# Projections of the next chunk moved inside the recurrence of the current one, recurrence in half steps, and three smaller edits

## What is computed

```python
# 1. state space block (the mixer)
h = rmsnorm(x); xi, z = split(h @ in_proj.T)             # 2 x 512 columns
xi = silu(causal_conv(xi, 4 taps))
dt, B, C = split(xi @ x_proj.T)                          # 16 + 16 + 16
delta = softplus(dt @ dt_proj.T + b); A = -exp(A_log)    # 512 channels, 16 states
s = s * exp(delta*A) + delta*B*xi                        # over tokens
y = (sum over states of s*C + xi*D) * silu(z)
x = layernorm(2*x + y @ out_proj.T)
# 2. cross attention: 8 heads, rotary on q and k, 2 x 64 keys, then relu(norm(.) @ W_ffn)
x = layernorm(x + xattn(x, ctx))
# 3. mixture of experts: one shared and 8 routed, top 2 by softmax
x = layernorm(x + sum_e c_e * (silu(x @ w1_e + b1) * (x @ w3_e + b3)) @ w2_e)
```

## Time and profile before

| | us |
|---|---|
| median of 2 runs (lowest, highest) | 1169.16 (1169.08, 1169.25) |
| profiled execution: its own time, its span | 1168.82, 1167.0 |
| busy in the span: PE, DVE, ACT, POOL | 916.1, 828.9, 545.8, 535.4 |

### The profile page before, as it was taken

The page is one execution under the profiler, slowest core; times in us unless marked ns, Lnnn a source line. Parts: engine busy times, 40 slices in busy tenths (PEclk is TensorE's granted clock), DMA queues, the critical chain, the costliest instruction groups (busy, mean ns, idle before and its releaser), DMA issues.

```text
span 1167.0 us, 13071 instructions
## 1 busy us (share of the span) xinstructions
PE 916.1 (79%) x4208; PEld 697.8 (60%) x4208; DVE 828.9 (71%) x1222; ACT 545.8 (47%) x1015; POOL 535.4 (46%) x318
## 2 busy tenths in 40 slices
PE   4857688486788998486788998477789985767996
PEld 2446673265677883265677883265678872645885
DVE  1699964698999954698999954698999961213233
ACT  3556736453455526453455526453555512413342
POOL 1267710743468720743468720743468723001552
PEclk9979999796689999796689999796689996755998
DMA  5111102101033302101033302102033212001330
GB/s 202 38 36 55 37 1 74 54 19 64 28 104 114 92 10 92 54 19 64 28 102 112 95 10 92 54 19 64 28 100 103 88 36 91 0 1 37 102 123 29
DMA packets 37714, 71.96 MB, mean 62 GB/s; under 512 B 3856, under 2 KB 12185, under 8 KB 37647
## 3 DMA queue, kind: packets, MB, share of 16 engines
q1 hardware_dynamic: 37646, 71.13, 18.9%
HBM read 64.62 MB, written 2.30 MB: 57 GB/s over the span
## 4 chain that ended last, share of the span: by engine, by line
PE 28%; issue 20%; POOL 19%; DVE 13%; ACT 5%; POOLq 0%; DMA 0%; DVEq 0%; ACTq 0%; SPq 0%
POOL dbu L537 11%; PE ps L928 8%; PE ps L1005 5%; DVE hs L1111 3%; POOL work L572 3%; PE ps L902 3%; PE ps L759 2%; DVE yacc L1164 2%; PE ps L848 2%; POOL w_lo L564 2%; DVE mx L1260 2%; POOL work L558 2%; POOL work L554 2%; PE ps L842 1%; ACT work L707 1%
## 5 line engine op out<-in xcount | busy, mean ns | idle before, releaser
L537 POOL TENSOR_TENSOR dbu<-v,bbc 128x1024 f32<-128x1024 f32 x128 | 301.8, 2364 | 218.0 <-DVE v L1097 124.4
L1111 DVE TENSOR_TENSOR_SCAN hs<-ps,carry,dbu 128x512 f32<-128x512 f32 x256 | 312.9, 1265 | 0.6 <-PE ps L759 0.6
L645 ACT ACTIVATE ps<-delta,neg_a 128x512 f32<-128x512 f32 x256 | 175.2, 691 | 174.0 <-DVE hs L1111 174.0
L759 PE MATMUL ps<-ident,hs 128*128 128x128 f32 x1024 | 161.2, 303 | 65.9 <-DVE yacc L1164 47.5
L759 PEld LDWEIGHTS ps<-ident,hs 128*128 128x128 f32 x1024 | 133.8, 158 | 90.5 <-DVE hs L1111 64.1
L564 POOL TENSOR_TENSOR w_lo<-w13s,w_hi 128x512 fp32r<-128x512 f32 x72 | 93.4, 1297 | 130.4 <-ACT w_hi L734 129.2
L1164 DVE SCALAR_TENSOR_TENSOR yacc<-ps,ctok,yacc 128x512 f32<-128x512 f32 x210 | 147.3, 737 | 1.9 <-PE ps L759 1.0
L1005 PE MATMUL ps<-w2s,work 128*128 128x256 f32 x576 | 136.3, 380 | 0.3
L747 ACT ACTIVATE work<-ps,half_b 128x512 f32<-128x512 f32 x72 | 49.6, 689 | 143.8 <-PE ps L928 139.8
L1005 PEld LDWEIGHTS ps<-w2s,work 128*128 128x128 f32 x576 | 105.8, 190 | 14.9 <-DVE work L1282 1.5
L928 PE MATMUL ps<-x_hi,w_hi 128*128 128x512 f32 x288 | 108.4, 458 | 7.6 <-DVE work L1282 7.3
(11 more groups left out here) (169 smaller groups left out, 1322.4 us busy)
## 6 DMA issues: line engine op xcount, KB each, us to landing
w13s<-in_w SPq DMA_DIRECT2D x72, 256.0 KB, 2.9
bbc<-brow_dram SPq DMA_DIRECT2D x32, 512.0 KB, 4.0
w2s<-in_w SPq DMA_DIRECT2D x36, 256.0 KB, 2.7
cbc<-comb_dram SPq DMA_DIRECT2D x32, 256.0 KB, 3.5
work<-work SPq DMA_DIRECT2D x16, 256.0 KB, 2.3
xn<-in_x SPq DMA_DIRECT2D x4, 512.0 KB, 4.7
xt<-in_x SPq DMA_DIRECT2D x4, 512.0 KB, 4.8
rope<-in_rope_q SPq DMA_DIRECT2D x4, 512.0 KB, 5.4
```

What stands on the lines that cost most here:

```text
L537: pool.tensor_tensor(dbu[:, i % DRING, :, :], v[:, 2 * h:2 * h + 2, :], bbc[:, n // 2 % 2, n % 2, :].rearrange("p (o t) -> p o t", o=1) .t ...
L645: act.activation(ps[:, unit % 2, :], delta[:, q, :], ACT.Exp, scale=neg_a[:, q * NS + m:q * NS + m + 1]).then_inc(da_done.sem, 1)
L759: last = pe.transpose(ps[:, bank, t * P:(t + 1) * P], src(t), ident[:, :])
L1111: dve.tensor_tensor_scan(hs[:, m % 2, q, 0:TC], ps[:, unit % 2, :], dbu[:, n % DRING, q % 2, :], carry[:, m, q:q + 1], ALU.mult, ALU.add). ...
```

## The change

The list is written anew. A recurrence now has 70 **half steps**, each with one unit and one sum. The `pre` steps of chunks 1 to 3 become twelve steps `ahead` 0 to 11, which stand inside the recurrence of the chunk before: in the first recurrence three half steps apart, later at the ticks 12 to 22 of the second stream, of 1.5 half steps each (attention ticks have 1, expert ticks 2). They use two or four PSUM banks and the buffer `work`, so their results (`u`, `sz`, `delta`, `v`, 1 MB each) are stored in DRAM (`kept`) and loaded back by `load` 0 to 2 towards the end of the recurrence and after `post` 3. Ticks of the second stream that don't fit in a recurrence are `left`: some stand at the boundary between two recurrences, two of them (`INSIDE`) in the next one.

The three smaller edits: the expert weights are split once, in the first recurrence, and the parts kept in DRAM, from where each chunk loads both (512 KB a half instead of 256 KB, ring of 4 instead of 3); the scores' factor is put in the keys, so that one reduction with `negate` gives `top` and L1263 goes; `gm` becomes `(b + b3)*gac` in PSUM and `hh = (th + 1)*gm`, so that neither has two operands in SBUF.

```diff
+UNITS = NS * Q
+STEPS = UNITS + 6
+WAITS = (1, 1, 1, 1, 1, 1, 1, 1, 1, 1, 1, 1, 1.5, 1.5, 1.5, 1.5, 1.5, 1.5, 1.5, 1.5, 1.5, 1.5, 1.5)
+LEFT_W, FIRST_W, FFN_W, INSIDE = 2, 4, 2, 2
...
+        for h in range(STEPS):
+            steps.extend(early[h] + mixer(i, "sum", h) + mid[h] + mixer(i, "scan", h) + late[h])
+            if h == STEPS - 8:
+                steps.extend(mixer(i + 1, "load", 0))
...
+    items = [only(3, mixer(0, "split", n)) for n in range(3)]
+    items += [only(3, mixer(1, "fetch", n) + mixer(0, "split", n + 3)) for n in range(4)]
+    items += [only(3, mixer(1, "ahead", n) + mixer(0, "split", n + 7)) for n in range(AHEAD)]
...
+        steps += mixer(i - 1, "post", 0) + mixer(i - 1, "post", 1) + mixer(i - 1, "post", 2) + mixer(i, "begin", 0)
+        steps += mixer(i - 1, "post", 3) + mixer(i, "load", 2)
...
+                if kind == "load" and n == 0:
+                    sp.wait_ge(*dbu_done.at(j, 0))
+                    sp.wait_ge(*dv_kept.at(j - 1, 128))
+                    sp.dma_start(v[:, :, :], kept["v"].rearrange("q p t -> p q t")).then_inc(v_in.sem, 16)
...
-                sp.dma_start(w13s[:, c % HRING, :, :, :].rearrange("p s k n -> p (s k n)"), w13[c]
-                             ).then_inc(w13_in[c % HRING].sem, 16)
+                sp.wait_ge(*b_ps.at(j, max(0, c - HRING + 1)))
+                for dst, src in ((w13_hi, hi_dram), (w13_lo, lo_dram)):
+                    sp.dma_start(dst[:, c % HRING, :, :, :].rearrange("p s k n -> p (s k n)"), src[c]
+                                 ).then_inc(w13_in[c % HRING].sem, 16)
...
+                    if c == 0 and j + 2 < CHUNKS:
+                        pe.wait_ge(*delta_done.at(j + 2, Q))
...
-                        dve.tensor_reduce(mx[:, :], s8, AX.X, ALU.max).then_inc(mx_done.sem, 1)
-                        dve.tensor_scalar(top[:, :], mx[:, :], -HD ** -0.5, None, ALU.mult
+                        dve.tensor_reduce(top[:, :], s8, AX.X, ALU.max, negate=True).then_inc(top_score_done.sem, 1)
...
-                    dve.scalar_tensor_tensor(out=gm[:, ib, :], in0=th[:, ib, :], scalar=1.0,
+                    dve.wait_ge(*b_ps.at(j, c + 1))
+                    dve.scalar_tensor_tensor(out=ps[:, 5, :], in0=ps[:, 5, :], scalar=col("b3", c),
                                              in1=(gac if c >= 2 else ga)[:, ib, :],
                                              op0=ALU.add, op1=ALU.mult).then_inc(gm_done.sem, 1)
```

More of the change, by code:

```diff
@@ new lines, in mixer, with second, tick, round_of @@
+    def mixer(chunk, *what):
+        return [("mixer", chunk, *what)] if 0 <= chunk < CHUNKS else []
+    def second(chunk, t, *parts):
+        return [("second", chunk, part, t) for part in parts]
+    def tick(chunk, t, weight, more=()):
+        return weight, second(chunk, t, "early"), second(chunk, t, "mid"), second(chunk, t, "late") + list(more)
+    def round_of(i, items):
+        early, mid, late = ([[] for _ in range(STEPS)] for _ in range(3))
+        at = 0.0
+        for weight, e, m, l in items:
+            start, end = int(at), max(int(at), int(at + weight) - 1)
+            early[start] += e
+            mid[start] += m
+            late[end] += l
+            at += weight
+        assert at <= STEPS, at
+        for h in range(STEPS):
+            steps.extend(early[h] + mixer(i, "sum", h) + mid[h] + mixer(i, "scan", h) + late[h])
+            if h == STEPS - 8:
+                steps.extend(mixer(i + 1, "load", 0))
+            if h == STEPS - 6:
+                steps.extend(mixer(i + 1, "load", 1))
@@ L104, in schedule @@
+    steps += mixer(CHUNKS - 1, "post", 0) + mixer(CHUNKS - 1, "post", 1) + mixer(CHUNKS - 1, "post", 2)
+    for n in range(max(3, len(left))):
+        steps += mixer(CHUNKS - 1, "post", 3 + n) if n < 3 else []
+        steps += second(CHUNKS - 2, left[n], "early", "mid", "late") if n < len(left) else []
+    for t in range(T_OUT + 1):
+        steps += second(CHUNKS - 1, t, "early", "mid", "late")
     return steps
@@ L1099, in mixer @@
[L1099 to L1102 removed]
+                    tokens_of_c(j, 7)
+                    soft_start(j, range(Q))
+                if kind == "pre" and n == 6:
+                    soft_end(j, (0, 1))
+                    soft_end(j, (2, 3))
+                if kind == "sum" and 6 <= n < UNITS + 6:
+                    sum_states(j, *divmod(n - 6, NT))
@@ L1103, in mixer @@
+                if kind == "scan" and n < UNITS:
+                    for unit in (n,):
                         m, q = divmod(unit, Q)
```

540 lines of the change are left out of this document (381 added, 159 removed).

## The result

| | us |
|---|---|
| before, median of 2 runs (lowest, highest) | 1169.16 (1169.08, 1169.25) |
| after, median of 2 runs (lowest, highest) | 1299.94 (1299.63, 1300.25) |
| ratio, 95% interval | 1.1112 (1.1088 to 1.1136) |
| forecast, range | 1136 (1082 to 1190) |

The account below looks back on a forecast made before the run. Neither DVE (215.6) nor PE (214.1) fills a 262.8 us round; the gap moves between stages. 61.8 + 135.8 + 259.7 + 253.7 + 210.2 + 213 = 1134.2 us of span, forecast 1136, range 1082 to 1190.

Parts of the forecast that it names:

- What the change takes out of DVE: DVE's work per round: L1263 saves 5 us and `gm` 8 us, so 215.6 becomes 203.
- What moves, work and lock: Projections moved into the recurrence: 19.6 us of DVE work a chunk, plus 5 us of waiting beside POOL.
- third rival: DVE and POOL lock paid in full: 16 instructions wait 2.1 us each, 34 us a chunk, 1217 us; chance 0.07.
- First recurrence: First scan to gate's end: 106.2 plus 19.6 + 5 moved and 5 for waits, 135.8 us; splits and DMAs hide.
- Start and rotary step: Start of each round: 18.8 + 25.6 us in round 1, 6.3 + 25.6 in rounds 2 and 3; rotary step uncovered.
- Tiles: Attention tiles: PE is late at 7.6 us a tile, 32 us in rounds 1 and 2, 30 in round 3.
- Ticks 12 to 22: Norms, gate and projections: 73 us in rounds 1 and 2, between 64 overlapped and 90 in a row; 34.5 in round 3.
- second rival: In ticks 12 to 22 the two chains run one after the other, 90 us instead of 73 twice, 1170 us; chance 0.20.
- Experts: Expert ticks: PE bounds at 5.35 us each, 85.6 us in round 1, 96.3 in round 2; DVE bounds round 3, 106.7.
- Boundary: Between two recurrences: 24.7 us from last sum to chunk 2's first scan, 11 idle on DVE; 20.5 in round 2.
- fourth rival: A store or load comes late at each boundary, 5 to 10 us a round; a stall dear as the lock had 0.05.
- The rest: From chunk 3's output projection to the end: 215.1 us before becomes 213.

Follow-up runs that it names:

- e4_two_edits: The kernel before with only the one reduction with negate and `gm` in PSUM; median of five runs 1149.5 us against 1170.1, ratio 0.9824.
- e5_wide_ahead: The kernel after with 2.5 half steps in place of 1.5 in each of ticks 12 to 22; 1298.6 us.
- e1_no_ahead: The kernel after without `ahead`, its `fetch` and the stores and loads of results, chunks 1 to 3 using what chunk 0 left; 1149.9 us.

## Why the prediction was wrong, step by step

**What the change takes out of DVE: right.** `gm` has come down to 0.73 to 0.76 us, and `e4_two_edits` alone gains 10.3 us in each of the first two rounds.

**What moves, work and lock: right.** 25.8 us of DVE in the first recurrence against my 24.6. The group of convolution instructions in after, beside POOL:

```profile
L1431 DVE SCALAR_TENSOR_TENSOR work<-work,vec 128x512 f32<-128x512 f32 x36 | 39.0, 1148 | 3.3 <-ACT work L861 3.1
```

1.15 us each instead of 0.75 makes 14.4 us in three chunks, 4.8 a chunk; I took 5. `v` takes 0.90 us on average and costs no more than before's 0.96. The rule on the lock (the Trainium skill, "SBUF — State Buffer", section "Who interferes with whom") names the mechanism, the trace agrees with single instructions of up to 2.84 us here, and its worst case, my third rival, is not what made the kernel slow.

**First recurrence: wrong by 47.7.** The step that failed is "I allow 5 for waits between engines" and "they and their DMAs hide". The waits were 31.6 (57.4 less 25.8), the splits 11.2, and the half steps, which I had at nothing, 8.5. Busy times of 68 and 69 us on ACT and POOL said that they have room, not that the room lies where a block of 5 us can stand. Of the waits the table loads are 13 and the places within a step 6. Some 12 are left, if these add up, and what holds them stays open; halving PE's products didn't shorten it. That these steps have two PSUM banks at a time, where the projections of before had four, was not tried apart.

**Start and rotary step: right, too low by 7 in rounds 2 and 3.** The hole before the first reduction came (8.6 us on PE and 4.3 to 6.2 before the first cosine).

**Tiles: wrong by 15 each time.** "Here PE is late next, 7.6 us a tile" priced PE's work. The step that failed is to take PE's work as the length: PE was busy for 36.9 of 47.2 us. What fits all runs is that, once DVE has less to do, the tiles last as long as the chain of a tile through DVE, ACT and PE, with the clock's share open as said. Its length stood in before's trace at 990.72 to 1036.14, 45.4 us, in the very stream from which I had taken the rotary step's 25.6.

**Ticks 12 to 22: wrong by 14 twice, and the top two left out.** The step that failed is "the stage is 73 at a third of that way". A third of the way between full overlap (64) and one after the other (90) was a choice without a row, and the 90 has none either: the two chains as given, 33.5 and 37, add up to 70.5. 87 were measured. With the top two, the stretch takes 47.5 us without projections, and these add 39.6 in a row and 45.0 woven in: the moved chain is paid in full, as my second rival had it. The argument against it (DVE has 64 us of other work there) doesn't hold: by `e5_wide_ahead` DVE's work doesn't set the length, since 16 us more of it made the stretch 6.6 longer. In round 3, where nothing runs ahead, the stage was right (35.7 for 34.5). The top two are a plain omission: I took them out of the norms in rounds 1 and 2 and put them nowhere, and with them the lead-in to the first `gm`, 13.7 us together. Of these 6.6 come back in the experts, which I counted from an earlier tick (79.0 and 89.7 for 85.6 and 96.3).

**Experts: right in rounds 1 and 2, 7 too low in round 3.** Ticks of 5.35 us with PE full in rounds 1 and 2, 5.5 in round 3; the parts from DRAM never came late: PE idles for 0.5 us in the experts of round 1, and as long in those of round 2. They bought no time either, since `e4_two_edits`, which splits anew, has the same ticks.

**Boundary: 4.3 too low and 1.9 too high.** 29.0 and 18.6 against 24.7 and 20.5. The late store or load, my fourth rival, didn't show: without any of them (`e1_no_ahead`) the first boundary takes 28.9 (411.84 to 440.69).

**The rest: 4.4 too low.** The first `gm` now waits for the product `b` as well (the `b_ps` line of the diff): from the top two's reciprocal to the first `gm` it is 7.1 us (1201.42 to 1208.53), where before had 1.6 (1071.36 to 1072.92). The ticks behind it take 2.8 us less.

So the mistake was one of kind: I summed work per engine and gave the dependent chains a share of overlap. The moved chain cost its bare length at all three places, and more; the finer order, which I gave no price, lost 4 to 12 us at each stage where undoing it is shown above. Small slips in the sums (the parts of the first boundary make 24.5, the case's own range 1113 to 1160) change nothing in this.

## What to carry to other kernels

Before moving a dependent chain beside another one, read the bare length of both in the trace, at a place where each runs alone; in this kernel, with queues worked off in order and two or three buffers between engines, idle time of an engine was no room for a chain, and the sum of the bare lengths would have been the safer forecast. Ask also what the moved chain had covered at its old place. Independent work in the gaps of a stage that waits can be cheap there (16 us of DVE work for 6.6, the scans in the tiles for nothing that shows), so that taking it out may buy nothing. Edits that shorten a single instruction on the engine that is full (here two, 10 us a round) can be tried without the restructuring that they came with.

## What was not expected of the hardware

Eight table loads of 1.28 us on ACT cost 13.2 us in the first recurrence, and 4.1 between the attention norm and the top two. The Trainium skill, "ScalarE: Activation LUTs", section "Table sets: the hidden batching unit", says that one set holds both Exp and Ln; here Ln (L854) and the return to Exp (L855) each load a table, twice a chunk, so half of the loads may be avoidable; no run here tried it.

The same kind of products of the input projection, eight in a row, took PE 3.70, 3.60, 5.87 and 3.70 us in ticks 12 to 22 of round 1 (timeline of after, the second and the third):

```profile
340.27 3.60 PE L1042 MATMUL ps<-work,win 128*128 128x512 f32 x8
...
353.79 5.87 PE L1042 MATMUL ps<-work,win 128*128 128x512 f32 x8 [0.94 <-ACT work L841]
```

The granted clock was 1.00 (2.4 GHz) from 337.32 to 345.00 us, 0.67 from there to 353.79, where PE worked 3.9 of 8.8 us, and 0.62 during the third eight, between this level and that of 1.2 GHz (0.50). So the chain behind a gap of PE can be slower than PE's busy time elsewhere says. It isn't always: in the first recurrence of after all four took 3.60 to 3.70 us, two of them after waits of 1.29 and 1.75 us.
